# Loop turns that begin inside the front half, and loads waited for where they are used

## What is computed

```
x = x + diag(softmax(Q K^T / sqrt(512), axis=1)) * V        # embedding attention, on layernorm(x)
x = x + two local layers, on layernorm(x):                  # depth 2
      h = h + windowed attention (8 heads of 64, windows of 64, look back one window,
              token shift, l2-normed q and k, rotary with xpos) @ wo
      h = h + (a * gelu(g)) @ w2, from layernorm(shifted h) @ w1, 341 hidden
x = x + causal attention of 16 heads of 8, on layernorm(x)
x = x + mixture of 8 experts, top 2 of 8 by softmax, plus one shared expert, on layernorm(x)
```

## Time and profile before

| | |
|---|---|
| median of 3 runs | 2063.85 us (2063.61 to 2066.46) |
| the profiled execution | 2061.38 us |
| its span, first to last instruction | 2059.3 us |
| mean granted TensorE clock | 0.91 |
| busy: PE, DVE, ACT, POOL | 1616.5, 1121.5, 1015.8, 605.5 us |

### The profile page before, as it was taken

The page is one execution under the profiler, slowest core; times in us unless marked ns, Lnnn a source line. Parts: engine busy times, 40 slices in busy tenths (PEclk is TensorE's granted clock), DMA queues, the critical chain, the costliest instruction groups (busy, mean ns, idle before and its releaser), DMA issues.

```text
span 2059.3 us, 32978 instructions
## 1 busy us (share of the span) xinstructions
PE 1616.5 (78%) x11554; PEld 941.5 (46%) x11632; DVE 1121.5 (54%) x2562; ACT 1015.8 (49%) x2297; POOL 605.5 (29%) x400
## 2 busy tenths in 40 slices
PE   1666688986889768895889868897699957898579
PEld 1334244553546435562445535463355625455235
DVE  3443492746646474644927466464837449274514
ACT  1435246653657327472466536573374724665041
POOL 5624060513315051420605033150515106051000
PEclk9787789997999889997999979999899979999689
DMA  4010200112002120113101120021201130011301
GB/s 127 19 23 1 59 23 2 50 51 62 21 1 65 50 47 21 28 46 77 31 2 49 51 62 21 1 65 51 47 21 34 49 79 20 2 49 44 62 2 51
DMA packets 37330, 80.69 MB, mean 39 GB/s; under 512 B 6766, under 2 KB 22638, under 8 KB 33760
## 3 DMA queue, kind: packets, MB, share of 16 engines
q1 hardware_dynamic: 37136, 78.22, 14.8%
HBM read 54.74 MB, written 8.78 MB: 31 GB/s over the span
## 4 chain that ended last, share of the span: by engine, by line
PE 43%; DVE 17%; ACT 14%; issue 13%; POOL 10%; DMA 1%; SPq 1%; DVEq 0%; POOLq 0%; ACTq 0%
PE ps L324 37%; PE ps L329 6%; ACT work L718 4%; DVE cmax L1032 4%; POOL work L1178 4%; ACT big L785 4%; POOL small L1155 3%; DVE small L934 2%; POOL work L1189 2%; DVE work L903 2%; ACT L807 1%; ACT L718 1%; ACT big L807 1%; DVE work L902 1%; DVE small L910 1%
## 5 line engine op out<-in xcount | busy, mean ns | idle before, releaser
L324 PE MATMUL ps<-bxt,mw 128*128 128x512 f32 x576 | 276.6, 604 | 3.7 <-ACT big L807 3.7
L324 PE MATMUL ps<-maskb,identb 128*128 128x128 bf16 (+1 forms) x1106 | 228.7, 239 | 27.9 <-ACT work L718 16.4
L718 ACT ACTIVATE work<-ps,pbias,small 128x128 f32<-128x128 f32 x512 | 226.1, 473 | 48.0 <-DVE pbias L938 47.5
L1155 POOL TENSOR_TENSOR brs<-bmv,consts 128x4 f32<-128x4 f32 x16 | 3.2, 202 | 754.3 <-DVE bmv L843 754.3
L324 PE MATMUL ps<-wqkv,h 128*128 128x512 f32 x384 | 199.4, 651 | 30.9 <-ACT v L680 11.0
L1032 DVE TENSOR_REDUCE cmax<-ps 128x1 f32<-128x384 f32 (+3 forms) x352 | 204.3, 630 | 29.7 <-PE ps L324 29.6
L1178 POOL TENSOR_TENSOR work<-work 128x1024 f32<-128x1024 f32 x64 | 150.7, 2354 | 232.2 <-DVE work L903 231.6
L1155 POOL TENSOR_TENSOR small<-small,consts 128x8 f32<-128x8 f32 x128 | 208.2, 1640 | 2.6 <-DVE small L912 2.6
L324 PE MATMUL ps<-pk,pq 96*128 96x512 bf16 (+3 forms) x512 | 139.6, 329 | 79.6 <-DVE cmax L1032 54.7
L329 PE MATMUL ps<-ident,work 128*128 128x128 f32 x1056 | 169.4, 307 | 40.0 <-DVE work L979 12.9
L785 ACT ACTIVATE big<-ps 128x512 f32<-128x512 f32 x320 | 163.9, 634 | 57.0 <-PE ps L324 56.9
(11 more groups left out here) (162 smaller groups left out, 2611.0 us busy)
## 6 DMA issues: line engine op xcount, KB each, us to landing
mw<-in_experts SPq DMA_DIRECT2D x72, 384.0 KB, 3.0
pk<-scr_parts SPq DMA_DIRECT2D x48, 192.0 KB
pq<-scr_parts SPq DMA_DIRECT2D x144, 64.0 KB
v<-v SPq DMA_DIRECT2D x16, 512.0 KB, 4.5
v<-v SPq DMA_DIRECT2D x16, 384.0 KB, 5.8
scr_parts<-big SPq DMA_DIRECT2D x8, 768.0 KB, 3.9
xin<-in_x SPq DMA_DIRECT2D x8, 256.0 KB, 4.4
out<-x SPq DMA_DIRECT2D x8, 256.0 KB, 3.1
```

Source lines behind the costliest of these rows:

```text
L324: return nc.tensor.matmul(o, a, b, start=start, stop=stop, skip_group_check=True)
L718: i = nc.scalar.activation(pr[:, m, a, p, :], fb[2 * (m % 2) + a][:, p * P:(p + 1) * P], ACT.Exp, bias=pbias[:, m, k:k + 1], scale=rn[:, m ...
L1155: return nc.gpsimd.tensor_tensor(out, x, consts[:, k:k + 1].broadcast_to([x.shape[0], x.shape[1]]), op)
```

## The change

It cuts the front half in generators `embed`, `project` and `attend`, on every engine, and joins them anew: `enter(s)` is the embedding and the first part of local layer 0; `leave(s)` is the rest, from the attention of layer 0 to `x2`. Ahead of the loop run enter(0), leave(0) and enter(1), alone. Six turns hold leave(t+1) and then enter(t+2), merged with back(t). A seventh, outside the loop, holds leave(7) beside back(6), by the same strings with the missing steps left out. Then comes back(7) alone. The strings of ORDER are new ones.

Because `x2` of the next sequence is now written while the back half of the present one still needs its own, ACT copies `x2` to `x2c` at the back half's beginning, and the residual add reads the copy. The add that writes `x2` waits for that copy and for the back half's first normalisation.

In the program's beginning the loads are grouped with a semaphore for each group, `xin` goes first, and each group is waited for at its first use; the staging of masks and rotary factors moves from the front half's `work` tiles to the back half's `ctmp` and `big`. DVE clears `pk` and sets its rows of ones, ahead of its first statistics; it scales the rotary factors after the first normalisation. ACT converts the masks. POOL clears `va` and `pq` between its two front norms of sequence 0.

```diff
+FRONT_ENTERED = 6
 ORDER = {
+    "tensor": "FBFBFFFFFFFFFFFFFBBBBFBBBBBBBBBBBBFBBFBBBFBFBBBFFBBBBFBBBBFBBBFBBFBBBFBBBBFBBBBFBBBBBBBBBBBBBBBBBFBB"
+        "FBBFFBBBBBFBFBBBFFBBBFBBFBBBBBBBBBBBBBBFBBBBFBBBBFBFBFFFFFFBFBBBBFBBBBBBFBBBFBBBBBFFFFBFFBFBBBFBBBFF"
+        "FBFFFFBBBBBBFBFFBFBFFFBFBFBBFFBBBFBFBFFB",
+    "scalar": "BFBFBFFFFFFFFFFFFFFFFFFFFFFFFFFFFFBBBBBBBBBBFFBBBBBBBBFBBBFFBBBBBBFBFBBBBFFBBBBBBBBBBBFFFBFFFBFFFFFF"
+        "FFBBBBBBBFBFFBBFFFBBFFBFFFFBBBFFFFFFBFFFFFBFFBFFBFF",
+    "vector": "BFBFBFBFBFBFFBFFFFFFFBBBBBBBBBBBFBBBBBBBBBBFFBBBBFBBBBFBBBBFBBBBFFFBBBBBBBBFFFBFFFFFFFFFFFFFFFBBFBBF"
+        "FFBFBFBBBBBBBBFBBBFBBBFFBBFFFBFFBFBFBFFFFBFFFBFBFFFBBFFBFFFFFFBBBFFBBFBFFB",
+    "gpsimd": "BFFFFFFFFFFFFFFFFFFFFFBFFFFFFFFFFFFFFF",
+    "sync": "BBBFBBFBBBBBBFB",
 }
...
+    for half in (enter(0), leave(0), enter(1)):
+        for _ in half:
+            pass
+    with engine.Fori(0, SEQS - 2) as t:
+        merge(chain(leave(t + 1), enter(t + 2)), back(t))
+    merge(leave(SEQS - 1), back(SEQS - 2))
     for _ in back(SEQS - 1, last=True):
         pass
...
+            def enter(s):
+                yield from embed(s)
+                yield from project(s, 0)
+
+            def leave(s):
+                yield from attend(s, 0)
+                for l in range(1, LAYERS):
+                    yield from project(s, l)
+                    yield from attend(s, l)
                 yield "out"
...
         def _(pe):
-            pe.wait_ge(loaded, 16 * n_loads)
+            pe.wait_ge(loaded_embed, 16 * len(embed_loads))
             pe.wait_ge(ready_v, 1)
-            pe.wait_ge(ready_p, 2)
...
                 yield f"qk0.{l}"
+                if is_first(s):
+                    pe.wait_ge(loaded_local[l], 16)
...
                 yield "tp2"
+                if is_first(s):
+                    act.wait_ge(ready_p, 1)
                 act.wait_ge(f_tp.sem, f_tp.at(s, 2))
                 nc.scalar.copy(h[0:64, 0:T], fb[0][0:64, :])
                 nc.scalar.copy(h[64:128, 1:T + 1], fb[0][64:128, :]).then_inc(f_xt.sem, 1)
+                if is_first(s):
+                    act.wait_ge(loaded_masks, 16)
+                    nc.scalar.copy(maskb[:, :], maskf).then_inc(ready_m, 1)
...
             def back(s, last=False):
+                yield "x2"
+                act.wait_ge(f_x2.sem, f_x2.at(s, 1))
+                nc.scalar.copy(x2c[:, :, :], x2[:, :, :]).then_inc(b_x2.sem, 1)
                 yield "tp"
...
         def _(dve):
-            dve.wait_ge(loaded, 16 * n_loads)
-            dve.wait_ge(x3_free, 16)
+            for r in range(2):
+                i = nc.vector.memset(pk[r][:, :, :], 0.0)
+            i.then_inc(ready_k, 1)
             nc.vector.memset(consts[:, 0:1], EPS)
             nc.vector.memset(ss[:, :, :, :], 1e-24)
+            nc.vector.memset(consts[:, 1:2], -0.5)
+            dve.wait_ge(ready_k, 1)
+            for r in range(2):
+                nc.vector.memset(pk[r][96:99, :, :], 1.0)
+            dve.wait_ge(loaded_embed, 16 * len(embed_loads))
+            cp(identb[:, :], ident[:, :])
+            ts(abq[:, :], ab[:, 0:1], float(T) ** -0.5, None, ALU.mult).then_inc(ready_v, 1)
             dve.wait_ge(ready_v, 1)
-            dve.wait_ge(ready_p, 2)
...
                 normalise(s, 1, xin, fxn, fmv, frs, f_rstd, f_xn)
+                if is_first(s):
+                    scale_rotary()
...
                 yield "out"
                 dve.wait_ge(f_ft.sem, f_ft.at(s, 1))
+                if not is_first(s):
+                    dve.wait_ge(b_x2.sem, b_x2.at(s - 1, 1))
+                    dve.wait_ge(b_xn.sem, b_xn.at(s - 1, 1))
                 tt_(x2[:, :, :], fb[3][:, :].rearrange("p (a b) -> p a b", a=NT), x1[:, :, :], ALU.add).then_inc(f_x2.sem, 1)
...
                 rstd(s, 1, f_stats, fmv, frs, fp, f_rstd)
+                if is_first(s):
+                    back_constants()
...
         def _(sp):
+            load_x(0)
+            for dst, src in embed_loads:
+                sp.dma_start(dst, src).then_inc(loaded_embed, 16)
+            for dst, src in rotary_loads:
+                sp.dma_start(dst, src).then_inc(loaded_rotary, 16)
+            sp.dma_start(wqkv[:, 0, :], io["wqkv"][0, :, :]).then_inc(loaded_local[0], 16)
+            sp.dma_start(maskf, io["masks"]).then_inc(loaded_masks, 16)
+            for dst, src in late_loads:
+                sp.dma_start(dst, src).then_inc(loaded_late, 16)
```

More of the change, by code:

```diff
@@ L13 @@
 from contextlib import ExitStack
+from itertools import chain
 import numpy as np
@@ L84, with run_turns, merge @@
 EXP_AT = exp_places()
[L87 to L93, removed]
+def run_turns(engine, order, enter, leave, back):
+    def merge(front, back):
+        halves = {"F": front, "B": back}
         for half in halves.values():
@@ L116, with start @@
 class Chain(Signal):
[L119 to L120 removed]
+    def start(self, k=0):
+        self.k = k
     def one(self):
@@ L639, in back, with embed @@
                 down(ALL - 1)
-            run_halves(pe, ORDER["tensor"], front, back)
+            run_turns(pe, ORDER["tensor"], enter, leave, back)
         @block.scalar
         def _(act):
-            def front(s):
+            def embed(s):
                 yield "tp"
@@ L807, in back @@
                         nc.scalar.activation(silu[e % 2][:, c, :], bb[n % 3][:, :], ACT.Silu).then_inc(m_silu.sem, 1)
-            run_halves(act, ORDER["scalar"], front, back)
+            run_turns(act, ORDER["scalar"], enter, leave, back)
         @block.vector
@@ L1131, in back @@
                 finish(bv)
-            run_halves(dve, ORDER["vector"], front, back)
+            run_turns(dve, ORDER["vector"], enter, leave, back)
         @block.gpsimd
@@ L1280, in back @@
                 sp.dma_start(out[bass.ds(s, 1), :, :].rearrange("o (a p) e -> p (o a) e", p=P), outb[:, :, :]).then_inc(x3_free, 16)
-            run_halves(sp, ORDER["sync"], front, back)
+            run_turns(sp, ORDER["sync"], enter, leave, back)
             sp.wait_ge(x3_free, 16 * (SEQS + 1))
```

826 lines of the change are left out of this document (428 added, 398 removed).

## The result

| | before | changed |
|---|---|---|
| median | 2064.95 us (2063.61 to 2066.46, 4 runs) | 1996.18 us (1995.35 to 1997.42, 4 runs) |
| the profiled execution, its span | 2061.38, 2059.3 us | 1997.42, 1995.6 us |

The changed kernel takes 0.9667 of the time before [0.965, 0.9684]: 3.3% less, where 4.6% was forecast. 1996.18 lies inside the range, 27 us above the forecast of 1969. The profiled execution is 30.8 us above its own forecast of 1966.6.

The account below looks back on a forecast made before the run. Bound: each turn starts with two latency chains and nothing dense beside them; PE is busiest, 78%. Start 15.6 + 194.6 + 54.1 + 6T + (T − 35) + 160.2, T = 225, gave span 1964.5, median 1969 us; range 1898 to 2032.

Parts of the forecast that it names:

- T: Length of one new full turn of the loop: forecast 225 us, ±9, with break-even at 238.5.
- PE work at full clock: PE's matrix work in one turn, the same after the change: 187 us.
- cost of the clock: Lower PE clock in a turn: 7 us in layer 0's attention, 2 in its feed-forward.
- idle, attention 0 and the jump: PE idle in layer 0's attention beside the back half's norm, projections and packing, including 4.3 of stops: 13 us.
- idle, feed-forward 0: PE idle in layer 0's feed-forward beside 31 of 44 score maxima, a DVE-bound stretch of some 25 us: 4 us.
- idle, dense part: PE idle over the remaining maxima, layer 1, exponentials, routing and four experts: 5 us.
- idle, entering: PE idle while the next sequence enters beside the last four experts, a 57 us stretch: 9 us.
- since at full clock the first stretch's own matmuls also end sooner, I take 225: Last step of the turn's sum: lowered it from 227 to 225 us for the first stretch's matmuls.
- what the seventh turn lacks: Turn without entering: loses its 57 us but runs four experts alone, some 22, so 35 us shorter.
- Edits at nothing: Rotary scaling, POOL's clears, mask conversion and x2 copy were said to fit idle or covered time, adding nothing.
- The start: Program start to first statistics: 15.6 us, bounds 8 and 23, set by DVE's four memsets; 27.0 before.
- The packing rival: New first stretch waits for packed operands: margin 3 us, slower only if the split comes 17 late; chance 0.06.

Follow-up runs that it names:

- old_turns: Changed kernel's start and copy of x2, but the loop's turns and ORDER strings of the kernel before; 2050.93 us, ratio 0.9938 to the kernel before.
- enter_serial: Changed kernel with every engine's entering steps moved behind its last expert of the turn; 2165.98 us, ratio 1.0496 to the kernel before.
- before_again: The kernel before, unchanged, profiled once more to see its turn lengths; 2067.55 us in one execution.
- clears_early: Changed kernel with POOL's clears of va and pq moved ahead of its first front norm; 1989.66 us, ratio 0.9644 to the kernel before.
- unrolled: Changed kernel with its six loop turns written out, without the hardware loop; 1963.22 us, ratio 0.9512 to the kernel before.
- packing_late: Changed kernel with DVE's splits of the packed parts moved behind the second set of probabilities; 2039.61 us, ratio 0.9891 to the kernel before.

## Why the prediction was right, and where it was off

**The mechanism.** That a turn starts with two chains of latency and nothing dense beside them, and that moving the border cures this, is confirmed from both sides: the two waits of 9.0 and 8.3 are gone, `old_turns` leaves about 55 of the 69 us to the border, and `enter_serial` loses them again, and more.

**The size of T.** Forecast and measured ledgers of a turn, the latter from the six windows above (this turn is the shortest of the five that a jump ends):

| | forecast | measured |
|---|---|---|
| PE work at full clock | 187 | 190.0 |
| cost of the clock | 7 + 2 | 8.7 |
| idle, attention 0 and the jump | 13 | 10.5 + 2.2 |
| idle, feed-forward 0 | 4 | 1.8 |
| idle, dense part | 5 | 7.1 |
| idle, entering | 9 | 7.5 |
| sum | 227 | 227.8 |

The work is busy time by clock, row for row. Of its 3 us too much, the 78 matmul records that the earlier trace rows lacks explain one: ten of them belong to the turn of the earlier trace rows, and a turn of `before_again`, whose trace lacks none, gives 187.9 by windows cut alike. The other 2 are open; a mean clock times busy time over a wide stretch is not exact. Single lines are off by up to 3 us and offset each other, and against the mean of the five turns, 229.2, the ledger is 2 short. With that it was right. The step that failed is the one behind it, "since at full clock the first stretch's own matmuls also end sooner, I take 225". The first stretch runs at 0.79, and its clock was already a term of the sum.

Over the seven turns (21.8 us too many) it comes apart by the jump, all from the distances above:

| | forecast | measured | times | difference |
|---|---|---|---|---|
| a turn without its jump | 220.7 | 222.1 | 7 | +9.8 |
| jumps | 7 × 4.3 | 5 × 7.1 | 1 | +5.6 |
| what the seventh turn lacks | −35 | −28.6 | 1 | +6.4 |

The first line is the 2 us taken off, 14 in all, less 0.6 a turn that the ledger was too long. The second: I counted the stop in every turn, but six turns have five jumps, and each costs more than its stop. The third hides behind the agreement of 193.5 − 228.05 = −34.6 with −35: no jump touches the seventh turn, so it is to be held against 222.1, and then the entering part is worth 28.6.

**"Edits at nothing".** This is the other step that failed. "The back half's clears run on POOL between its two front norms, where it idled 17.82" looked at POOL alone. The cover was there, but POOL's work stopped DVE on the critical path: 7.4 us that the sum had at nothing, where it stood. `clears_early` wins 6.5 of the median back by another place alone. The other edits at nothing did cost a little: without the stop, in `clears_early`, sequence 0 still takes 197.5 us from its first statistics to `x2`, against 194.6 in the kernel before and 195.5 in `before_again`. Which edit these 2 to 3 us belong to was not tested.

**The start.** 14.3 against 15.6. Each memset of ones took 3.47 us, so POOL's 3.51 was a fair stand-in; each zeroing took 1.76, on 2048 elements of uint32. The trace agrees with the possibility that the Trainium skill gives for zeros (VectorE: DVE Perf Modes, "Zero memsets can be issued as uint32 (trn2)"). By the Trainium skill's one cycle per element at 0.96 GHz (same page), which I had worked out to a start of 14.1 (14.0 when the sum is done again), a memset of ones would be an estimated 4.27 us. The trace has 3.47, so the rule is too slow here, and 14.1 came near by luck: stops between the memsets make up for it.

**The jump.** The stop stays, as forecast, and I counted 4.3 for it. Its length on DVE is 4.5 to 6.9, 5.1 on average; a jump costs 7.1. The other 2 are longer busy time of PE at a slightly lower clock, by the windows under `unrolled`; why the clock is lower there was not tested.

**The packing rival** was given a margin of 3 us; the traces give nearly 5. The forecast's turn includes the stop, so from the stop's beginning: the split was placed at 21 us and its store came at 21.2 (16.6 from 732.31), the data were placed at 40 and came at 37.7, and PE's need, placed at 43, came at 42.7.

**The range** of 1898 to 2032 held the result. Its upper end, T = 234, is what `packing_late` reaches with 233.7.

## What to carry to other kernels

Where a loop turn begins with chains of latency, look for dense work at its end to put them beside, and check that they are then really interleaved: the border alone makes nothing faster, and here the interleaving decided between 1996 us and 2166. When an edit is moved into an engine's idle time, look what the other engines do then, on DVE and POOL above all: idle time of POOL is not free time of DVE. And when a ledger of a stretch closes, take its sum: a correction for an effect that already has its own line counts it twice.

## What the hardware did that I had not expected

- DVE's `tensor_scalar` of 128 columns (fp32) and its cast stand nearly still beside POOL's clears: 1.11 to 8.53 and 8.90 us for a group of four, 0.23 to 2.07 for a cast. One such instruction can stand through several of POOL's (8.32 us). A `tensor_scalar` of one column did not (0.14). POOL's own clears were hardly slowed (7.12 and 6.99 for two).
- A bf16 memset of zeros in 4096 columns ran as 2048 of uint32 in 1.76 us; one of ones, on 3 rows, took 3.47.
- The loop's jump stops DVE for 4.5 to 6.9 us a turn in the new order and PE for up to 4.5, and a jump costs 7.1 in one order of work and 3.5 in another; 2.2 and 0.7 of these are longer busy time of PE, not idle time.
- The same program has turns 2.8 us longer, with a clock of 0.50 to 0.54 and not 0.61 in the fourth 10 us behind the write of `x2`, two in one execution and three in another.
